# Local layers: two PSUM banks for the q/k projections in turn, denominators before values, and three stage entries rearranged

## The reference, cut to what matters

```
x = x + favor(layernorm(x))       # stage 1: 16 heads, random features, causal linear attention
x = x + router(..); x = x + cosine_attention(..); x = x + int4_linear(..)
x = x + mamba(layernorm(x))       # state-space scan over 256 steps, 16 states
x = x + experts(..); x = x + hgrn(..)
x = x + local(layernorm(x))       # six layers:
for i in range(6):
    q, k, v = split(shift_tokens(x) @ Wqkv[i])            # 16 heads of 64
    q, k = rotary(l2norm(q) * qs), rotary_inv(l2norm(k) * ks)
    attn = softmax(mask(8 * q @ k.T))                     # a key sees its window of 32
    x = (attn @ v) @ Wo[i] + x
    a, gate = split(layernorm(shift_tokens(x)) @ W1[i] + b1[i])
    x = (a * gelu(gate)) @ W2[i] + b2[i] + x
```

## Time and profile before

| | us |
|---|---|
| median of 3 runs (lowest, highest) | 6519.71 (6516.19, 6521.88) |
| the profiled execution | 6522.74 |
| its span, first to last instruction | 6520.8 |

### The profile page before, as it was taken

The page is one execution under the profiler, slowest core; times in us unless marked ns, Lnnn a source line. Parts: engine busy times, 40 slices in busy tenths (PEclk is TensorE's granted clock), DMA queues, the critical chain, the costliest instruction groups (busy, mean ns, idle before and its releaser), DMA issues.

```text
span 6520.8 us, 129965 instructions
## 1 busy us (share of the span) xinstructions
PE 5878.9 (90%) x51681; PEld 3219.8 (49%) x51681; DVE 4384.8 (67%) x7178; ACT 3402.6 (52%) x5560; POOL 2289.2 (35%) x1597
## 2 busy tenths in 40 slices
PE   7999878999677778998689999999999999999998
PEld 3555554444422225765445555555555555555554
DVE  4656434454288894334678888888878788887885
ACT  3444324656144443444456656666666666665664
POOL 0111101222034441000055555555555555555553
PEclk9999978999688888998799999999999999999998
DMA  5555302333100000000011111111111111111110
GB/s 138 115 115 119 89 0 53 80 82 83 44 3 0 0 0 1 1 0 1 24 36 32 40 43 34 31 47 37 34 45 38 33 44 40 34 39 41 38 37 24
DMA packets 298945, 275.95 MB, mean 42 GB/s; under 512 B 40580, under 2 KB 289572, under 8 KB 298148
## 3 DMA queue, kind: packets, MB, share of 16 engines
q1 hardware_dynamic: 298372, 268.00, 17.7%
HBM read 30.88 MB, written 2.10 MB: 5 GB/s over the span
## 4 chain that ended last, share of the span: by engine, by line
PE 33%; issue 5%; DVE 5%; POOL 5%; ACT 2%; DMA 0%; POOLq 0%; DVEq 0%; SPq 0%; ACTq 0%
PE banks L2254 7%; PE banks L2289 6%; PE banks L2324 5%; PE banks L2309 4%; PE banks L2267 3%; PE banks L2341 3%; DVE local_probs L2559 2%; POOL local_rot L2653 2%; POOL local_ssum L2645 2%; PE banks L2363 2%; PE banks L2313 2%; PE banks L2274 1%; ACT local_probs L2455 1%; DVE local_gate L2584 1%; DVE local_sin L2540 1%
## 5 line engine op out<-in xcount | busy, mean ns | idle before, releaser
L2645 POOL TENSOR_TENSOR local_ssum<-local_sq 128x512 f32<-128x512 f32 x384 | 697.5, 1816 | 2145.1 <-ACT local_sq L2433 2144.6
L2653 POOL TENSOR_TENSOR local_rot<-local_rot,local_inv_all 128x512 f32<-128x512 f32 x768 | 964.6, 1288 | 94.1 <-DMA local_inv_all<-local_inv 93.6
L2254 PE MATMUL banks<-local_y,local_Wqkv 128*128 128x512 f32 x1536 | 823.0, 618 | 64.0 <-ACT local_sq L2433 61.2
L2559 DVE TENSOR_TENSOR local_probs<-banks,band 128x576 f32<-128x576 f32 x768 | 546.2, 753 | 185.4 <-PE banks L2289 180.1
L2455 ACT ACTIVATE local_probs<-local_probs,local_npeak 128x1152 f32<-128x1152 f32 x384 | 482.8, 1257 | 357.1 <-DVE local_probs L2559 357.1
L2539 DVE TENSOR_TENSOR local_rot<-banks,local_rotary_scaled 128x512 f32<-128x512 f32 x768 | 525.6, 684 | 191.1 <-PE banks L2254 185.6
L2433 ACT ACTIVATE local_sq<-banks 128x512 f32<-128x512 f32 x768 | 459.4, 598 | 253.6 <-DVE local_sin L2540 244.8
L2546 DVE TENSOR_TENSOR local_rot<-local_rot,local_sin 128x1024 f32<-128x1024 f32 x384 | 513.7, 1338 | 41.9 <-DVE local_sin L2540 2.3
L2449 ACT COPY local_v<-banks 128x512 f32<-128x512 f32 x384 | 224.9, 586 | 594.1 <-PE banks L2267 593.6
L2289 PEld LDWEIGHTS banks<-local_rot 32*128 32x128 f32 x12288 | 416.7, 186 | 225.0 <-issue 200.8
L2540 DVE TENSOR_TENSOR local_sin<-banks,local_rotary_scaled 128x512 f32<-128x512 f32 x768 | 522.4, 680 | 0.0
(11 more groups left out here) (400 smaller groups left out, 10561.4 us busy)
## 6 DMA issues: line engine op xcount, KB each, us to landing
local_inv_all<-local_inv SPq DMA_DIRECT2D x768, 128.0 KB, 2.7
favor_half_norm_all<-favor_half_norm SPq DMA_DIRECT2D x512, 128.0 KB, 3.0
cosine_inv_all<-cosine_inv SPq DMA_DIRECT2D x256, 128.0 KB, 2.6
favor_rden<-favor_inv SPq DMA_DIRECT2D x256, 64.0 KB, 2.1
cosine_rden<-cosine_inv_den SPq DMA_DIRECT2D x256, 64.0 KB, 2.1
local_Wqkv<-in_L_ffn_Wqkv_quads SPq DMA_DIRECT2D x36, 256.0 KB, 2.9
local_Wo<-in_L_ffn_Wo_quads SPq DMA_DIRECT2D x6, 512.0 KB, 4.1
experts_w_W<-in_L_ffn_W SPq DMA_DIRECT2D x1, 2048.0 KB
```

The source lines that it names most:

```text
L2254: pe.matmul(seqs(banks[:, QK_BANK, :]), Wqkv[:, at:at + P], y_group(g), start=True, stop=True).then_inc(qk_projected, 1)
L2559: dve.tensor_tensor(probs[:, e % 3, r:r + 2, :], banks[:, S_BANK + r:S_BANK + r + 2, 0:SCORES], consts["band"].unsqueeze(1).broadcast_to([ ...
L2645: pool.tensor_tensor(ssum[:, n % 2, m, :], sq[:, 0, :], sq[:, 1, :], ALU.add).then_inc(square_summed, 1)
L2653: pool.tensor_tensor(a, a, twice(inv_all[:, n % 2, m, of_seq(s)]), ALU.mult).then_inc(united, 1)
```

## The change

In `local_layers`: projections with even number use bank 0, those with odd number bank 1; the v projection stays in bank 1, between an even and an odd one; denominators move to bank 0 and are made ahead of the values. ScalarE's `take_den` is parted into `log_den`, placed ahead of the `exp` of the same half step, and `invert_den`. Waits follow. The scaled tables of a layer are made in two parts. The first block normalises group 0 alone; groups 1 to 7 are done in steps 0 to 6. In `state_space` the next group's statistics, normalise, transposes and copy come four steps earlier (the last four steps of the group before that), `project_out` is parted over steps 3 and 4, `add_out` is at 5. In `build` the first block loads x, four constants and the favor weights; five constants and the weights of router, cosine, int4, mamba and hgrn (38 transfers) are issued by SyncE in favor's steps 1 to 6.

The core of the diff:

```diff
+    LOADS = 1
...
+                    if i == LOADS:
+                        for tile, source in w["later_consts"]:
+                            sp.dma_start(tile, source).then_inc(w["consts_loaded"][0], 16)
+                    if 0 < i - LOADS <= len(w["later"]):
+                        w["later"][i - LOADS - 1].load(sp)
+                sp.wait_ge(*w["consts_loaded"])
...
     MEASURE, NORMALIZE, TURN, TURNED, WIDEN, LOWER, BIAS, LOWER_C, BIAS_C, LAST_DT, SPLIT_ALL, SOFTPLUS, DELTA = \
-        0, 1, 2, 3, 5, 7, 8, 9, 10, 11, 12, 13, 14
-    GATE, WAY_OUT, ADD_OUT = 2, 3, 4
-    FIRST, LAST = -NS, N + ADD_OUT
+        -4, -3, -2, -1, 5, 7, 8, 9, 10, 11, 12, 13, 14
+    GATE, WAY_OUT, ADD_OUT = 2, (3, 4), 5
+    FIRST, LAST = MEASURE - NS, N + ADD_OUT
...
+                    if m:
+                        pe.wait_ge(dt_biased, CH * m)
...
-                def project_out(g):
+                def project_out(g, half):
                     pe.wait_ge(gated, CH * (g + 1))
-                    for t in range(GT):
+                    for t in range(half * GT // 2, (half + 1) * GT // 2):
...
-                    if (g := finish_at(k, WAY_OUT)) is not None:
-                        project_out(g)
+                    for half in range(2):
+                        if (g := finish_at(k, WAY_OUT[half])) is not None:
+                            project_out(g, half)
...
                     if m >= 2:
-                        act.wait_ge(out_ready, m - 1)
+                        act.wait_ge(out_ready, 2 * (m - 1))
...
                 def add_out(g):
-                    dve.wait_ge(out_ready, g + 1)
+                    dve.wait_ge(out_ready, 2 * (g + 1))
...
-    QK_BANK, V_BANK, S_BANK, O_BANK, X_BANK = 0, 1, 2, 6, 7
+    DEN_BANK, V_BANK, S_BANK, O_BANK, X_BANK = 0, 1, 2, 6, 7
     LAST = QUADS * (MLPS - 1) + 13
...
+    qk_bank = lambda c: (DEN_BANK, V_BANK)[c % 2]
...
-        rows = room[:, TILES * D:TILES * D + DEPTH * 2 * HD].rearrange("p (l m d) -> p l m d", m=2, d=HD)
+        rows = room[:, 0:DEPTH * 2 * HD].rearrange("p (l m d) -> p l m d", m=2, d=HD)
+        xn = y_last.rearrange("p (t d) -> p t d", d=D)
...
+        def measure(dve, g):
+            for tile in tiles_of(g):
+                dve.bn_stats(ln_stats[:, tile, :], x[:, tile, :]).then_inc(stats_done, 1)
+            for tile in tiles_of(g):
+                dve.wait_ge(stats_done, tile + 1)
+                dve.bn_aggr(ln_moments[:, tile, :], ln_stats[:, tile, :]).then_inc(moments_done, 1)
+            dve.wait_ge(moments_done, GT * (g + 1))
+            dve.tensor_scalar(ln_var[:, g * GT:(g + 1) * GT], ln_moments[:, g * GT:(g + 1) * GT, 1], LN_EPS, None, ALU.add).then_inc(var_done, 1)
+
+        def root_x(act, g):
+            of_g = slice(g * GT, (g + 1) * GT)
+            act.wait_ge(var_done, g + 1)
+            act.activation(ln_log[:, of_g], ln_var[:, of_g], ACT.Ln).then_inc(log_done, 1)
+            act.wait_ge(log_done, g + 1)
+            act.activation(ln_rstd[:, of_g], ln_log[:, of_g], ACT.Exp, scale=-0.5).then_inc(rstd_ready, 1)
+
+        def normalize_x(dve, g):
+            dve.wait_ge(rstd_ready, g + 1)
+            if g:
+                dve.wait_ge(turned, g)
+            for tile in tiles_of(g):
+                dve.tensor_scalar(xn[:, tile % GT, :], x[:, tile, :], ln_moments[:, tile, 0:1], ln_rstd[:, tile:tile + 1],
+                                  ALU.subtract, ALU.mult).then_inc(normed, 1)
+
+        def turn_x(pe, g):
+            pe.wait_ge(normed, GT * (g + 1))
+            for tile in range(GT):
+                last = pe.transpose(banks[:, X_BANK, tile * P:(tile + 1) * P], xn[:, tile, :], consts["ident"])
+            last.then_inc(turned, 1)
+
+        def copy_x(act, g):
+            act.wait_ge(turned, g + 1)
+            for side, a in y_sides(g):
+                act.copy(a, seqs(banks[side, X_BANK, :])).then_inc(y_ready, 1)
...
+                measure(dve, 0)
...
+                normalize_x(dve, 0)
...
+                root_x(act, 0)
+                copy_x(act, 0)
...
+                turn_x(pe, 0)
...
-                    if c:
-                        pe.wait_ge(squared, c)
+                    if half:
+                        pe.wait_ge(v_copied, c // 2 + 1)
+                    elif n >= 3:
+                        pe.wait_ge(den_logged, 2 * n - 5 + m)
+                    elif c:
+                        pe.wait_ge(squared, c - 1)
...
+                        if layer == 0 and quad == 0:
+                            pe.wait_ge(y_ready, 2 * (g + 1))
...
                     at = quad * QUAD_COLUMNS + (c % 4) * P
-                    pe.matmul(seqs(banks[:, QK_BANK, :]), Wqkv[:, at:at + P], y_group(g), start=True, stop=True).then_inc(qk_projected, 1)
...
-                    if j >= 6:
-                        pe.wait_ge(den_logged, j - 5)
-                    elif j:
-                        pe.wait_ge(v_copied, j)
+                    if j:
+                        pe.wait_ge(squared, 2 * j)
...
+                    at_step = n + 2 + s
                     pe.wait_ge(exped, e + 1)
+                    if at_step < N:
+                        pe.wait_ge(squared, 4 * at_step + 3 - 2 * s)
+                    elif e:
+                        pe.wait_ge(den_logged, e)
+                    for lo, hi, tile in ((0, BAND, 0), (BAND, SCORES, 1)):
+                        for r in range(4):
+                            at = tile * P
+                            last = pe.matmul(banks[32 * r:32 * r + 32, DEN_BANK, at:at + hi - lo], consts["ones"][:, 0:32],
+                                             probs[:, e % 3, r, lo:hi], start=(tile == 0), stop=(tile == 1), skip_group_check=True)
+                    last.then_inc(den_summed, 1)
                     pe.wait_ge(v_copied, min(e + 6, 2 * N))
-                    if e + 6 > 2 * N:
-                        pe.wait_ge(den_logged, e)
                     if e:
                         pe.wait_ge(normalized, e)
-                    for part in range(3):
+                    for part in range(2):
...
+                    if 1 <= i < GROUPS:
+                        take_x(y_ready, 2 * (i + 1))
+                        turn_x(pe, i)
...
-                def take_den(e):
-                    act.wait_ge(valued, e + 1)
+                def log_den(e):
+                    act.wait_ge(den_summed, e + 1)
                     if e >= 2:
                         act.wait_ge(normalized, e - 1)
-                    act.activation(rden[:, e % 2, :], banks[:, V_BANK, 0:SEQ], ACT.Ln, scale=UP).then_inc(den_logged, 1)
+                    act.activation(rden[:, e % 2, :], banks[:, DEN_BANK, 0:SEQ], ACT.Ln, scale=UP).then_inc(den_logged, 1)
+
+                def invert_den(e):
                     act.wait_ge(den_logged, e + 1)
                     act.activation(rden[:, e % 2, :], rden[:, e % 2, :], ACT.Exp, bias=up_full[:], scale=-1.0).then_inc(rden_ready, 1)
...
+                    if (e := within(2 * (i - 3) + 1)) is not None:
+                        log_den(e)
                     if (e := within(2 * (i - 2))) is not None:
                         exp(e)
                     if i < N:
                         square(4 * i + 1)
                     if (e := within(2 * (i - 3) + 1)) is not None:
-                        take_den(e)
+                        invert_den(e)
...
+                    if 1 <= i < GROUPS:
+                        copy_x(act, i)
+                    if (e := within(2 * (i - 2))) is not None:
+                        log_den(e)
                     if (e := within(2 * (i - 2) + 1)) is not None:
                         exp(e)
+                    if i < GROUPS - 1:
+                        root_x(act, i + 1)
                     if (G := mlp_at(i, 8)) is not None:
                         square_mlp(G)
                     if (G := mlp_at(i, 9)) is not None:
...
                     if (e := within(2 * (i - 2))) is not None:
-                        take_den(e)
+                        invert_den(e)
...
-                def scale_tables(layer):
-                    for m in range(2):
...
+                def scale_tables(layer, m):
+                    for half in range(2):
+                        scale = scales[:, layer, 2 * m + half:2 * m + half + 1]
...
+                    if n % STEPS == 0 and half == 0:
+                        dve.wait_ge(tabled, 8 * layer_of(n) + 4 * m + 4)
...
+                    dve.wait_ge(valued, e + 1)
...
                     if i < N:
+                        if i == 0:
+                            scale_tables(0, 0)
+                        rotate_start(4 * i)
                         if i % STEPS == 0:
-                            scale_tables(i // STEPS)
-                        rotate_start(4 * i)
+                            scale_tables(i // STEPS, 1)
...
+                        if i % STEPS == STEPS - 1 and i < N - 1:
+                            scale_tables(i // STEPS + 1, 0)
```

(17 more changed lines are left out.)

71 lines of the change are left out of this document (23 added, 48 removed).

## The result

The changed kernel takes 6562.29 us (median of 4 runs, 6557.97 to 6564.55) against 6517.95 before: ratio 1.0065, 95% interval 1.005 to 1.008. It is slower by 44 us; forecast was 6552, slower. Its profiled execution took 6561.64 us, span 6559.7.

The account below looks back on a forecast made before the run. TensorE in `local_layers` (busy 3034.4 of 3108.9 us) was taken as the bound. 6522.7 + 85 (local steady) − 24 (entry to local) − 20 (stage 1) − 9 (state space) = 6554.7 profiled, so 6552 median; range 6425 to 6590.

Parts of the forecast that it names:

- The second half of a step: Local body: exp queues behind a log awaiting denominators; variance matmul waits 1.23 us, gate matmul 1.29 us, each period.
- The bare first half: Local, one step in four; P starts projection 4i+1: v projection waits 0.33 us (0.43 without prefetched weights), replacing 0.70.
- the sum: Local body, idle per period: 0.43+1.23+1.29+0.35 = 3.3 us, 3.4 with a remainder of 0.1, against 1.59 before.
- The norm: Local, step with the widen matmuls: norm matmul waits 0.35 us for GpSimd's sum, late through the square of 4i+3.
- Body and drain: Local's steady steps, 47 periods with 3.4 us idle against 1.59: +85 us, bounds +64 and +109.
- Steps 0 to 6: Start of local, normalising groups 1 to 7: banks win some 7 us in the first three, steps 3 to 5 cost +3.5.
- the entry: Entry to local, first block (−22 us) and steps 0 to 6 together: −24 us, bounds −16 and −31.
- Stage 1: First copy 24 us earlier, x load landing 13.3 us after issue, 4 us given back: −20 us, bounds −12 and −24.
- The banks win: Rival for local: exp's wait for denominators does not reach TensorE, q/k bank waits go; 6436 us, chance 0.24.
- The rotation loop becomes the bound: Rival for local: norm, inverse, copies, unites, sum loop adds 1.2 us a period; 6608 us, chance 0.07.
- Local costs but others absorb it: Rival: +64 us in local, −64 from entries at their better ends (−24, −22, −18); 6520 us, chance 0.11.
- the entries: Places where stages start: entry to local −24 us, stage 1 −20 us, state space −9 us.

Follow-up runs that it names:

- run 1: Changed kernel with the log of the even denominators, in the second half of a step, behind the exp and the MLP operation: 6455.41 us, ratio 0.9906 to the kernel before.
- run 2: As run 1, but the exp of the odd scores still waits for the even denominators: 6542.16 us, ratio 1.004 to the kernel before.
- run 11: Kernel of Run 5 with the first half's log of the odd denominators behind the exp too: 6452.69 us, ratio 0.9902 to the kernel before.
- run 6: Changed kernel with one q/k bank, denominators behind the values in bank 1 and ScalarE's old order; entry edits stay: 6481.48 us, ratio 0.9943 to the kernel before.
- Run 5: Changed kernel with second-half log_den behind the square of 4i+3, and stage 1's 43 later loads issued one a step: 6452.21 us, ratio 0.9898 to the kernel before.

## Why the prediction was right

**The second half of a step: right, shown.** The log that waits for denominators, the exp behind it, the MLP operation behind both: waits of 1.23 and 1.29 us were forecast, 1.28 (60.0 over 47) and 1.25 (57.3 over 46) measured. Counted by starts against run 1, where they are gone, the two places are 1.32 us longer each. Run 1 takes them away by ScalarE's order alone, run 2 brings most of them back by a wait alone.

**The bare first half: right, size nearly.** The square ended at P+3.84 (forecast 3.82), and the v projection starts right behind it, at P+3.89 (3.87). The view of waits calls only 0.1 us of this a wait; the starts tell more. In run 11, where the v projection waits for nothing, it follows projection 4i+2 after 0.96 us and the scores follow after 0.95; in the changed kernel it is 1.22 and 1.06. The wait therefore costs 0.26 + 0.11 = 0.37 us a period where the sum had 0.43 (0.33 and 0.1 for weights not fetched ahead). The one term that was off is the 0.86 in "TensorE alone would have it at P+1.06+0.61+1.01+0.86 = 3.54": it was taken from two wide matmuls that follow wide ones, and behind narrow ones it is 0.96.

**The norm: right size, wrong engine.** Forecast were 0.35 us behind GpSimd's sum; it is 0.34 in a good period (0.51 in the mean of 41 waits) behind VectorE's last MLP product of the step, which the late gate pushes back. In run 1, without the late gate, a good period has no such wait.

**Body and drain: +87.7 against +85.** The idle time is the forecast one: 159.5 over 47 is 3.39 a period, 3.4 was the sum. A good period has 1.27+1.25+0.34+0.10 = 2.96 of it (0.76 before); the starts of layers (9.9 us at the widen matmul) and longer waits of the norm make up the rest. That the total comes out so near is in part luck: the sum had 0.43 at the v projection, of which the view counts only 0.10 as idle, and no cost for the late tables at the starts of layers (last section), and these offset each other. Two more things do: TensorE's busy time in the body is 7.7 us longer, and the drain behind it takes 67.4 us where it took 72.3.

**Steps 0 to 6: wrong by 4.6 us.** The forecast priced groups 1 to 7 at +3.5 us in steps 3 to 5 and a gain of 7 by the banks in the first three (that is −3.5; its total of −24 for the entry leaves −2). The 7 are real (run 6). What failed is "2.6 us on VectorE" for a group: its busy time in this stretch rose by 25.9 us (73.86 to 99.77), not 18. The 24 normalising operations take 0.77 us in the mean and not 0.34, since ten of them started beside a GpSimd operation and took 1.3 us:

```profile
3209.63 4.94 DVE L2201 TENSOR_SCALAR local_gate<-x,local_mlp_sq,local_mlp_yc 128x128 f32<-128x128 f32 x4
```

That is 9 to 10 us that the forecast did not have (the mechanism is in the last section). With 99.8 of 105.6 us VectorE is the bound in nearly all of these steps, not in three of them.

**Stage 1: −18.7 against −20.** The x load landed 11.3 us after its issue and not 13.3, so the first copy is 1.5 us earlier than forecast. The give-back is 6.8 us, not 4. Run 5 shows that it comes from loads bunched behind the copies of norms. Whether SyncE's time or the order inside the DMA queue did it stays open: one load a step relieves both. By the rule of the Trainium skill, "DMA: Bandwidth & Descriptors", that the prediction weighed, the term would have been −15; the measurement lies between.

**The rivals.** "The banks win" (6436) was right about the banks and wrong about the order: with ScalarE's order mended they do win, 6455 (run 1) against 6481 with one bank (run 6; 24 us by the ratios). The report in the Trainium skill, "TensorE: Matmul & The Clock Gate", that a second PSUM buffer gave nothing does not carry over to this kernel. "The rotation loop becomes the bound" did not happen in the changed kernel, which is too slow for it; it happened as soon as the queue was mended. "Local costs but others absorb it" took −24, −22 and −18 for the entries, which are not the bounds that the prediction gives for them (−31, −24, −25); the entries together measured −51.4 with steps 0 to 6 at +2.6 on top, so they did not absorb local's +87.7.

## What to carry to other kernels

An operation put at the head of an in-order queue brings its own wait along, and everything behind it pays: list the operations behind it and their slack (here 0.1 us) before moving it. A view of waits can hide a wait in what it calls busy (here 0.27 us in each bare first half): compare the starts of the same instructions in two runs. A producer and its log may move early only where the log's input is there before the next operation's; otherwise leave the log behind the operations that are due. And once the first bound is gone, look at the loop across engines that had been hidden by it: here one reordering on GpSimd, which was busy for only a third of the span, gave 35 us.

## What the runs showed of the hardware

**Small VectorE operations beside GpSimd.** In the changed kernel, last step of a layer (time line, GpSimd and VectorE):

```profile
4819.65 1.30 POOL L2701 TENSOR_TENSOR local_ssum<-local_sq 128x512 f32<-128x512 f32 x1 [8.51 <-ACT local_sq L2472]
4819.74 1.36 DVE L2573 TENSOR_SCALAR local_rotary_scaled<-local_rotary,local_qk_scales 128x256 f32<-128x256 f32 x1
4821.02 0.34 DVE L2574 TENSOR_SCALAR local_rotary_scaled<-local_rotary,local_qk_scales 128x256 f32<-128x256 f32 x1
4821.20 3.84 POOL L2709 TENSOR_TENSOR local_rot<-local_rot,local_inv_all 128x512 f32<-128x512 f32 x3 [0.26 <-DMA local_inv_all<-local_inv]
4821.28 1.36 DVE L2573 TENSOR_SCALAR local_rotary_scaled<-local_rotary,local_qk_scales 128x256 f32<-128x256 f32 x1
4822.57 1.35 DVE L2574 TENSOR_SCALAR local_rotary_scaled<-local_rotary,local_qk_scales 128x256 f32<-128x256 f32 x1
```

A table operation takes 0.34 us, in the kernel before always (48 of 48). Started beside a GpSimd operation of 1.3 us it takes 1.36 and ends just behind it; in the gap between two (4821.02) it takes 0.34. The normalising operations of steps 0 to 6 show the same: 0.34 us alone, 1.3 beside GpSimd. The Trainium skill, "SBUF — State Buffer", section "Who interferes with whom", says that a `tensor_scalar` in its two-port mode and GpSimd exclude each other for a whole instruction; the rows agree. The change put the tables in that place, and the prediction had no cost for it: it said only that half of them leave the layer start and that this is in its sums. The five periods with a start of a layer were together some 16 us over five good ones, before and after the change alike.

**A lower clock behind some idle times.** The late tables hold the widen matmul back by 2.78 us, and in the 5.5 us behind this wait the granted clock is 0.69 in the mean, between its two levels (1.2 and 2.4 GHz), where it was 1.00 before:

```profile
4740.00:4818.00 78.00, 74.52 (x855) 39.95 (x856) 62.17 (x87) 44.35 (x76) 33.79 (x26) 1.00 0.17 42
...
4825.00:4830.50 5.50, 5.27 (x53) 2.79 (x54) 5.40 (x9) 2.10 (x4) 1.27 (x2) 0.69 0.28 84
```

The 32 value matmuls there take 1.73 us and not 1.16. Periods with such a start of a layer are 72.2 to 72.8 us long where a good one is 68.15; three of the five are like this, and the clock fell in all three. In the other two one table is late and not three, TensorE idles 0.75 us, and the period is 69.4 at full clock. It does not happen every time: over all traces of this case, in the body of local, the clock fell to the lower level at 16 of 20 idle times of 2.6 to 2.9 us and at 7 of 20 of 2.0 to 2.56 us (in the kernel before, at two of its five of 2.12). What decides is not shown. The waits of 1.3 us in every step of the changed kernel did not do this: but for the three falls the clock of the body is 1.00.
